# Six small gaps between the SBUF tiles of a two-block cross-attention kernel

## The reference

```python
qh, kh, vh = qn @ Wq, kn @ Wk, vn @ Wv            # 256 -> 16 heads x 64
out = softmax((qh @ kh.T + bias) / 8) @ vh         # per head, 128 x 128
x = q + out @ fc_w.T + fc_b                        # 1024 -> 256
x = x + gelu(ln(x) @ W1.T + b1) @ W2.T + b2        # 256 -> 1024 -> 256
q, k, v = x @ Wq + bq, ctx @ Wk + bk, ctx @ Wv + bv    # 16 heads x 16, one kv head
attn = softmax(windowed(q @ k.T / 4)) @ v @ Wo + bo
gate = silu([attn, x] @ Wg + bg)
out = attn * gate + x * (1 - gate)
out = rms(out) * rms_w;  out -= out.mean(tokens)
```

## The kernel before, in words

| products | weights loaded from | moving from | moving minus loaded | by 128 |
|---|---|---|---|---|
| query projection | `wq` 16512 | `xT` 145792 | 1010 x 128 | 0 |
| key projection | `wk` 32896 | `cT` 149888 | 914 x 128 | 0 |
| value projection | `cT` 149888 | `wv` 49280 | -786 x 128 | 0 |
| fc | `OT` 164224 | `wfc` 65664 | -770 x 128 | 0 |
| MLP in | `w1` 82048 | `hT` 153984 | 562 x 128 | 0 |
| MLP out | `hidS` 205568 | `w2` 98432 | -837 x 128 | 0 |
| second block's query | `wq1` 114816 | `x2T` 213760 | 773 x 128 | 0 |
| output and gate | `o1T` 223232 | `wog` 119168 | -813 x 128 | 0 |
| gate of x | `x2T` 213760 | `wgx` 127360 | -675 x 128 | 0 |
| centring | `center` 137280 | `o1T` 223232 | 671.5 x 128 | 64 |

## Time and profile before

### The profile page before, as it was taken

The page is one execution under the profiler, slowest core; times in us unless marked ns, Lnnn a source line. Parts: engine busy times, 40 slices in busy tenths (PEclk is TensorE's granted clock), DMA queues, the critical chain, the costliest instruction groups (busy, mean ns, idle before and its releaser), DMA issues.

```text
span 1847.0 us, 55279 instructions
## 1 busy us (share of the span) xinstructions
PE 1814.7 (98%) x18702; PEld 1681.2 (91%) x18702; DVE 1483.5 (80%) x6755; ACT 1543.1 (84%) x5586; POOL 1294.0 (70%) x1324
## 2 busy tenths in 40 slices
PE   7999999999999999999999999999999999999997
PEld 5989999999999999999999999999999999999986
DVE  7778788887788887788887788887788887878774
ACT  5788888888888888888888888888888888889874
POOL 3656777766777766777766777776777776777754
PEclk9999999999999999999999999999999999999998
DMA  7434444444445444444444444444444444445432
GB/s 240 120 96 116 122 117 129 119 112 113 122 119 128 119 113 113 121 120 127 119 114 113 120 122 125 119 117 109 121 124 123 119 115 113 117 115 125 102 88 58
DMA packets 238059, 219.11 MB, mean 119 GB/s; under 512 B 48848, under 2 KB 220240, under 8 KB 237776
## 3 DMA queue, kind: packets, MB, share of 16 engines
q1 hardware_dynamic: 237776, 215.57, 45.4%
HBM read 71.29 MB, written 9.96 MB: 44 GB/s over the span
## 4 chain that ended last, share of the span: by engine, by line
PE 94%; DVE 3%; DMA 1%; ACT 1%; issue 1%; POOL 1%; SPq 1%; POOLq 0%; DVEq 0%; ACTq 0%
PE bank L611 12%; PE bank L613 11%; PE bank L612 11%; PE bank L625 9%; PE bank L629 8%; PE bank L626 8%; PE bank L785 7%; PE bank L798 7%; PE bank L910 4%; PE bank L923 3%; PE bank L621 3%; PE bank L617 3%; PE bank L618 3%; PE bank L635 2%; DVE soft L1749 1%
## 5 line engine op out<-in xcount | busy, mean ns | idle before, releaser
L2595 ACT ACTIVATE soft<-soft,row_min 128x128 f32<-128x128 f32 x1024 | 397.1, 391 | 66.1 <-DVE row_min L1749 65.9
L2515 ACT ACTIVATE soft<-soft,row_min 128x128 f32<-128x128 f32 x1024 | 398.5, 393 | 16.9 <-DVE row_min L1641 13.0
L3044 POOL TENSOR_TENSOR soft<-soft,inv_sum 128x512 f32<-128x512 f32 x256 | 271.8, 1062 | 170.6 <-DVE inv_sum L1649 170.5
L234 DVE STREAM_TRANSPOSE turned<-soft 128x512 f32<-128x512 f32 x512 | 342.0, 689 | 11.7 <-POOL soft L3053 4.1
L3053 POOL TENSOR_TENSOR soft<-soft,inv_sum 128x512 f32<-128x512 f32 x256 | 264.5, 1045 | 61.3 <-DVE inv_sum L1758 61.3
L1749 DVE CUSTOM_DVE_ANT_0 soft<-bank,winb 128x128 f32<-128x128 f32 x1024 | 230.4, 284 | 45.3 <-PE bank L910 38.2
L1641 DVE CUSTOM_DVE_ANT_0 soft<-bank,relb 128x128 f32<-128x128 f32 x1024 | 230.3, 283 | 21.8 <-PE bank L785 12.9
L2515 ACT ACTIVATION_READ_ACCUMULATOR soft<-soft,row_min 128x1 f32 x1024 | 194.4, 190 | 0.0
L2595 ACT ACTIVATION_READ_ACCUMULATOR soft<-soft,row_min 128x1 f32 x1024 | 193.0, 188 | 0.0
L785 PE MATMUL bank<-kT,qT 64*128 64x128 f32 x2048 | 148.7, 284 | 3.5 <-DVE kT L1621 0.5
L785 PEld LDWEIGHTS bank<-kT,qT 64*128 64x128 f32 x2048 | 125.0, 187 | 26.0 <-issue 20.8
(11 more groups left out here) (249 smaller groups left out, 6521.3 us busy)
## 6 DMA issues: line engine op xcount, KB each, us to landing
soft<-turned SPq DMA_DIRECT2D x1024, 128.0 KB, 2.7
tokens<-stats_by_row SPq DMA_DIRECT2D x63, 256.0 KB, 3.6
tokens<-in_x SPq DMA_DIRECT2D x32, 256.0 KB, 2.7
raw<-in_x_t SPq DMA_DIRECT2D x32, 256.0 KB, 3.2
x<-in_x SPq DMA_DIRECT2D x32, 256.0 KB, 2.7
out<-gate SPq DMA_DIRECT2D x63, 128.0 KB, 2.6
tokens<-in_ctx SPq DMA_DIRECT2D x31, 256.0 KB, 2.8
raw<-in_ctx_t SPq DMA_DIRECT2D x31, 256.0 KB, 2.7
```

The lines of the kernel that those rows point to most:

```text
L234: return eng.transpose(turned[:, slot, :, s % 2, :, :].rearrange("p j h b -> p h j b"), soft[:, s, :, :].rearrange("p h (j a) -> p h j a", ...
L2515: last = act.activation(soft[:, s, h, :], soft[:, s, h, :], ACT.Exp, bias=row_min[:, s, h:h + 1], scale=-1.0, accum_out=row_sum[:, s, h:h ...
L2595: last = act.activation(soft[:, s, h, :], soft[:, s, h, :], ACT.Exp, bias=row_min[:, s, h:h + 1], scale=-1.0, accum_out=row_sum[:, s, h:h ...
L3044: pool.tensor_tensor(soft[:, m % NS0, :, :], soft[:, m % NS0, :, :], inv_sum[:, m % NS0, :].unsqueeze(2).broadcast_to([P, QUAD, SEQ]), ALU ...
```

## The change

Six tiles that nothing reads or writes are put between the others. They move the start of all tiles behind them. The total grows by 352 bytes of a partition. No instruction, order, wait or size changes.

```diff
+        def skip(name, size):
+            sb(name, [P, size // 4])
+
         wq = sb("wq", [P, 2, KD, F], F32R)
         wk = sb("wk", [P, 2, KD, F], F32R)
+        skip("ahead_of_wv", 64)
         wv = sb("wv", [P, 2, KD, F], F32R)
+        skip("ahead_of_wfc", 64)
         wfc = sb("wfc", [P, 2, NC_F, D], F32R)
         w1 = sb("w1", [P, 2, KD, F], F32R)
         w2 = sb("w2", [P, 2, NC_F, D], F32R)
+        skip("ahead_of_wq1", 64)
         wq1 = sb("wq1", [P, 2, KD, D], F32R)
+        skip("ahead_of_wkv1", 64)
         wkv1 = sb("wkv1", [P, KD, 2 * HD])
...
         rstd2 = sb("rstd2", [P, GROUP])
+        skip("ahead_of_xT", 32)
         xT = sb("xT", [P, 2, KD, TOK], F32R)
...
         V = sb("V", [P, GROUP, QW])
+        skip("ahead_of_OT", 64)
         OT = sb("OT", [P, 2, GROUP, QC, SEQ], F32R)
```

## The result

The changed kernel takes 1838.11 us (median of four runs, 1836.77 to 1839.27) against 1848.89 us before (four runs too). The ratio is 0.9942, with a 95% interval of 0.9924 to 0.9959: 10.8 us faster, where 70 were forecast. The sign was right, the size was off by more than six times, and the range (from 1752 to 1862) held the time only because it reached over the rivals. In a later comparison, with five runs, the same kernel gave 0.9936 (0.9923 to 0.9948).

A forecast was written before the change was run, and what follows sets the result against it. PE was taken as the bound, the time being the sum of distances between matmul starts. From 1848.9 us, 90 us came off for shorter fp32r products and 20 us went back for hand-offs: 1779 us, range 1752 to 1862.

The forecast's parts named there:

- the rivals: Outcomes besides the forecast's 1779 us (0.48): small relief 1834 (0.13), no change 1849 (0.18), worse 1903 (0.21).
- the stall lies in the meeting of two reads: fp32r products: 11 ns stall each, from reading the moving operand and the next product's weights at once.
- I take 274 ns, the shortest that a regular fp32r product shows: 256-column fp32r products, 10,136 in all, fall to 274 ns: 88 us, with the 512-column ones 90 us together.
- The bound of 272 ns (113 us): Best case: fp32r products reach the fp32 duration of 272 ns, 113 us off including 512-column products.
- The products with 512 columns: 384 fp32r products with 512 columns go from 392 to 387 ns: 2 us faster.
- The give-back: Hand-offs from PE to ACT or DVE and back, about 14 places a group, take back 20 us.
- fp32, other engines, DMAs at nothing: fp32 products, ACT and DVE instructions and DMA moves counted as unchanged; up to 30 us kept for slower DMAs.
- the small relief: Rival: 32 acts as 64 or the odd kind, 281 ns; 15 us off, 1834 us; chance 0.13.
- the even kind: fp32r pairs starting an even number of 128 bytes apart, such as `w1` and `hT`: 7,680 products at 283 ns.
- the odd kind: fp32r pairs an odd number of 128 bytes apart (`hidS`, `x2T`, `center`): 2,456 products, medians 281 to 282 ns.
- Each collision already happens at D=0: Argument against the worse rival: the even kind's tight 283 ns looks like every possible collision already happening.
- worse: Rival: each line of the load meets the moving stream, products last 288 ns, 54 us slower, 1903 us; chance 0.21.

The follow-up runs named there:

- D=96: Kernel before plus seven gaps, so every fp32r pair's moving operand starts 96 bytes (by 256) from its loaded one: 1851.27 us, ratio 1.0006.
- The bare map: Whole computation left out, only fp32r products back to back at many start distances; 512 columns: 226.7 ns at 0, 233.4 at 32.
- D=32 everywhere: Kernel before with six gaps, so every fp32r pair has start distance 32 by 256, the MLP's two included: 1837.00 us, ratio 0.9929.

## Why the prediction was wrong

- *PE is the bound, and the stall lies in the meeting of two reads*: right as far as the runs go. The pace falls to 112 ns with one element moved and to 113.3 with half the columns loaded, and depends on D with no other engine at work. What exactly the two reads contend for isn't shown.
- *"I take 274 ns, the shortest that a regular fp32r product shows"*: this step failed. The term of 90 us measured 18. In the trace before, a duration of 274 is a single product within an uneven pattern (94 of `hidS`, which stand in a sequence 279, 274, 281, 287), and not a state in which a stretch stood. The fastest states seen, at D=112 and 192, have 275 and 276 on average. D=32 has a pattern of 113 to 120 with a mean of 117, and another of 117.8. The reason given, that reads which start in different places needn't yield, fails with D=96: 120.0 bare, and 1851.27 us in the whole kernel. That the two streams run past each other, so that 32 bytes at the start don't keep them apart, would fit, but no run separates it from other causes.
- *The bound of 272 ns (113 us)* was too far. The lowest pace at any D is 113.3 ns, 6.1 below the kernel's, so 62 us at most, and entries let D=192 have less than half of that.
- *The products with 512 columns*: forecast 2 us faster; their duration rose (392 to 397 ns) and their pace stayed (232.0 to 232.3), 0.1 us. The bare map (233.4 at 32, 226.7 at 0) doesn't carry over for them: in whole kernels D=32 everywhere gave 231.1 and D=0 232.6.
- *The give-back*: 20 of 90 us forecast, 7 of 18 measured. It isn't spread evenly over 14 places: one place has about half of it.
- *fp32, other engines, DMAs at nothing*: right, within the 2 us of DVE and the 0.1 us of `soft<-turned`.
- *The rivals*: the small relief (1834 us, 0.13) was the case that came. It named 281 ns for the even kind, which was 279 to 281. Its 15 us of products were 18, and it left out the give-back of 7, which is why it lies 4 us low. I gave it too little although the only rows with another distance, the ones at 64 and the odd kind, stood there. "Each collision already happens at D=0" was wrong as an exclusion of worse: D=4 takes 123.1.

## What to carry to other kernels

A stall that depends on addresses isn't removed by being apart; map it first with bare products over the distances that tiles can have, entered in many ways, since a long run may stand in a lucky pattern (D=112 gave 113.3 in one and 117.6 on average). Take such a gain from the mean of a state that rows show, not from the shortest single instruction. And in an order written by hand at a given pace of one engine, expect a good third of a faster pace to come back as waits at the places that have no margin, here 38 to 44%.

## What the runs showed of the hardware

- The pace of fp32r products with 256 columns depends on the start distance of the moving and the loaded operand by 256 bytes: 113.3 to 123.1 ns in the long runs. With 512 columns it is 226.7 to 234.3, and another distance is best (0, not 192); in the whole kernel that advantage of D=0 didn't show (232.6 ns against 232.0).
- The same instructions at the same distance hold one of two paces, 113.3 or 117.8 ns at D=192, for over a hundred products, depending on what came before. The same 48 instructions ahead led to either. Work of DVE, ACT, GpSimd and DMAs beside them changed neither.
- fp32 instructions with 256 columns don't show it: 215.8 ns at D=0 and at D=32, which are the two that were tried.
